# Routing tables by wide compares, and the last of the down weights' norms worked out inside the first tile

## What is computed

```python
x = x + xattn(layernorm(x), ctx)            # keys from ctx, similarity, layer norm over it, softmax
n = layernorm(x)
scores = n @ Wg.T                           # 8 experts
topk_s, topk_i = top_k(scores, 2);  probs = softmax(topk_s)
for e in range(8):                          # H = 352
    h = silu(n @ W1[e].T) * (n @ W2[e].T)
    y = y + w[..., e:e+1] * (h @ W3[e].T)
x = x + y
```

## Time and profile before

| what | value |
|---|---|
| median of 3 runs | 388.02 us (388.01 to 388.85) |
| the profiled execution's own time | 388.37 us |
| its span | 386.6 us |
| PE, DVE, ACT, POOL busy | 357.8, 272.8, 263.4, 163.6 us |
| mean granted PE clock | 0.961 of full |

### The profile page before, as it was taken

How to read it: one execution, slowest core, us unless ns; L and a number is a source line. 1 busy time by engine, 2 the same in 40 slices (tenths; PEclk the granted TensorE clock), 3 DMA queues, 4 the chain that set the end, 5 groups by cost and what they waited for, 6 DMA issues and landing times.

```text
span 386.6 us, 8316 instructions
## 1 busy us (share of the span) xinstructions
PE 357.8 (93%) x2317; PEld 235.7 (61%) x2317; DVE 272.8 (71%) x725; ACT 263.4 (68%) x455; POOL 163.6 (42%) x200
## 2 busy tenths in 40 slices
PE   8998999978979778889999999999999999999981
PEld 7554576756946445556666666666666666666640
DVE  2367788988796999995757676666767575757660
ACT  2388999966684988976666657575666666665750
POOL 2124748557334134545253434444343435253331
PEclk9999999998559899999999999999999999999998
DMA  6999999999412133355544445353535354544524
GB/s 226 412 409 401 323 412 388 367 339 357 162 19 66 31 54 57 54 86 88 103 68 98 77 91 84 82 89 77 101 67 109 61 105 68 98 76 91 81 31 54
DMA packets 21947, 57.62 MB, mean 149 GB/s; under 512 B 4816, under 2 KB 4944, under 8 KB 20368
## 3 DMA queue, kind: packets, MB, share of 16 engines
q0 software_dynamic: 8736, 20.53, 30.0%
q1 hardware_dynamic: 12016, 30.27, 20.8%
q10 hardware_dynamic: 1152, 6.29, 4.6%
HBM read 38.17 MB, written 18.91 MB: 148 GB/s over the span
## 4 chain that ended last, share of the span: by engine, by line
PE 73%; DVE 10%; issue 5%; ACT 4%; DMA 4%; POOL 2%; POOLq 0%; ACTq 0%; DVEq 0%
PE bank L1236 34%; PE bank L1270 17%; PE bank L1094 4%; PE bank L1227 4%; PE bank L1028 3%; PE bank L1256 3%; PE bank L1136 3%; DMA stage<-in_xT 2%; DVE stage L784 2%; PE bank L1114 2%; DVE stage L786 1%; DVE Wp L812 1%; PE bank L1121 1%; DMA out<-kvj_s,sidx 1%; ACT stage L660 1%
## 5 line engine op out<-in xcount | busy, mean ns | idle before, releaser
L967 DVE SCALAR_TENSOR_TENSOR stage<-W,w3sc,stage 128x512 f16<-128x512 f16 x117 | 84.2, 748 | 6.5 <-ACT stage L660 6.5
L1270 PE MATMUL bank<-stage,n_s 128*128 128x512 f16 (+1 forms) x351 | 82.2, 379 | 1.8 <-issue 1.5
L1236 PE MATMUL bank<-Wp,kvg_s 128*128 x480 | 78.2, 313 | 3.5 <-DVE kvg_s L973 3.5
L660 ACT ACTIVATE stage<-W,w3sc 128x512 f16 x117 | 80.1, 717 | 0.0
L1236 PE MATMUL bank<-Wp,kv_s 128*128 x456 | 75.9, 317 | 4.2 <-DVE kv_s L973 4.2
L506 POOL DMA_INDIRECT out<-oT_s,sidx x20 | 34.1, 1706 | 75.4 <-ACT oT_s L687 68.3
L1236 PEld LDWEIGHTS bank<-Wp,kvg_s 128*128 128x128 f16 x480 | 46.7, 98 | 29.6 <-issue 5.1
L1236 PEld LDWEIGHTS bank<-Wp,kv_s 128*128 128x128 f16 x456 | 44.9, 99 | 29.8 <-issue 5.5
L991 DVE TENSOR_TENSOR n_s<-bank,n_s 128x384 f16<-128x384 f32 x39 | 21.7, 557 | 55.1 <-ACT n_s L673 55.1
L506 POOL DMA_INDIRECT out<-kvj_s,sidx x19 | 32.4, 1707 | 65.7 <-ACT kvj_s L687 63.1
L1270 PEld LDWEIGHTS bank<-stage,n_s 128*128 128x128 f16 (+1 forms) x351 | 34.2, 98 | 35.1 <-issue 2.3
(11 more groups left out here) (184 smaller groups left out, 554.5 us busy)
## 6 DMA issues: line engine op xcount, KB each, us to landing
Wp<-in_w SPq DMA_DIRECT2D x8, 1408.0 KB, 10.8
W<-in_w ACTq DMA_DIRECT2D x8, 768.0 KB, 7.7
stage<-in_xT SPq DMA_DIRECT2D x4, 1024.0 KB, 9.8
W<-in_x SPq DMA_DIRECT2D x12, 256.0 KB, 10.9
out<-W SPq DMA_DIRECT2D x12, 256.0 KB, 8.7
n_table<-n_s SPq DMA_DIRECT2D x8, 256.0 KB, 7.2
n_table<-x_s SPq DMA_DIRECT2D x8, 256.0 KB, 5.5
stage<-in_x SPq DMA_DIRECT2D x4, 256.0 KB, 9.4
```

Source lines behind the costliest of these rows:

```text
L660: eng.activation(w3p[t % 2][:, c * D:(c + 1) * D], W3[:, bass.ds(e * W3N + c * D, D)], ACT.Copy, scale=w3sc[:, bass.ds(e, 1)]).then_inc(s_ ...
L967: eng.scalar_tensor_tensor(w3p[r][:, W3N + c * D:W3N + (c + 1) * D], W3[:, bass.ds(e * W3N + c * D, D)], w3sc[:, bass.ds(e, 1)], w3p[r][:, ...
L1236: mm = eng.matmul(bank[2 * which + r][:, 0:H], n_, w_, start=(c == 0 and k == 0), stop=(c == DC - 1 and k == 2))
L1270: mm = eng.matmul(ybank(t - 1)[:, :], h_, w_, start=(c == 0 and k == 0), stop=(c == HC - 1 and k == 2))
```

## The change

`columns(0..2)` become two DVE instructions each: one compare of 128x1024 against the ramp for `oh_r` and one for `oh_c`, with 16-bit copies of ri and qi repeated along the last axis. The multiplication by the row number moves to ACT as `number(q)`, four in-place activations of 128x256. Groups 3 and 4 stay as they were.

Order: `scale_in(15)` goes one slot ahead; `columns(0)` goes from slot 14 to slot 16, `places(1)` from 15 to 17, `columns(1)` from slot 16 to behind slot 17, `weight_sums` from 14 to 15, `weight_scale` from slot 16 to behind `chosen(12)`, POOL's `weight_root` from slot 14 to slot 17 (behind `norm(15)`). On ACT `w3_square(0)` goes from slot 14 to 15 and `w3_square(1)` behind `number(2)`; squares 6 and 7 go into `tile(0)`, with a junk buffer of their own. The matmul for W3's norms goes into PE's `tile(1)`, and `w3_sums`, `w3_scale` and the weights of tile 0's rows go into DVE's `tile(0)`, behind the gate and half a `w12_low`; ACT waits for `w3sc` in `w3_high` and no longer ahead of `tile(0)`. Fewer `warm` matmuls: 24 for 36 beside the gather, 8 for 12 in slots 14 and 15. The diff, cut to its core (`gate` and `row_weights` hold the instructions of L981 to L988 and L996 to L999, unchanged):

```diff
 W3_ORDER = (4, 5, 6, 7, 0, 1, 2, 3)
+W3_LATE = 6
 W3_LOAD_SLOT = (11, 12, 13, 14, 14, 15, 15, 16)
-WARM_GATHER = 36
+WARM_GATHER = 24
...
-WARM_LAST = 12
+WARM_LAST = 8
...
+WIDE = 3
...
+        rf16 = sb("rf16", [P, G * TOPK], F16)
+        qf16 = sb("qf16", [P, G * TOPK], F16)
...
+        w3junk.append(stage[:, DC * N:DC * N + W3N // 2].bitcast(BF16))
...
                     eng.memset(zrow[:, :], 0.0).then_inc(s_zr, 1)
-                if s == 14:
+                if s == 17:
...
-                if s in (14, 15):
-                    w3_square(s - 14)
+                if s == 15:
+                    w3_square(0)
+                if s == 16:
+                    number(0)
...
-                eng.activation(w3junk[k > 1], W3[:, e * W3N:(e + 1) * W3N], ACT.Square, accum_out=w3sq[:, e:e + 1]).then_inc(s_w3q, 1)
+                eng.activation(w3junk[(k > 1) + (k >= W3_LATE)], W3[:, e * W3N:(e + 1) * W3N], ACT.Square, accum_out=w3sq[:, e:e + 1]).then_inc(s_w3q, 1)
...
+            def number(q):
+
+                eng.wait_ge(s_ohp, q + 1)
+                for i in range(TPB):
+                    cols = slice(i * TOPK, (i + 1) * TOPK)
+                    eng.activation(oh_r[:, q % 2, cols, :], oh_r[:, q % 2, cols, :], ACT.Copy,
+                                   scale=tok1[:, q * TPB + i:q * TPB + i + 1]).then_inc(s_ohn, 1)
...
             turned(G - 2)
             router_exp(0)
+            number(1)
             turned(G - 1)
+            number(2)
+            w3_square(1)
             w12_high(0, 0)
+            w12_high(0, 1)
             w3_square(2)
-            w12_high(0, 1)
             w3_square(3)
             router_exp(1)
             eng.activation(spare_a[:, 1:2], half[:, :], ACT.Silu)
-            for k in range(4, E):
+            for k in range(4, W3_LATE):
...
                     wait(eng, s_yp, t - 1)
+                    eng.wait_ge(s_w3sc, 1)
                     eng.activation(w3p[t % 2][:, c * D:(c + 1) * D], W3[:, bass.ds(e * W3N + c * D, D)], ACT.Copy,
...
                 if t == 0:
                     mT_evac(1)
+                    for k in range(W3_LATE, E):
+                        w3_square(k)
+                    w12_high(EARLY, 0)
                 w3_high(t, e, 0)
-                w12_high(t + EARLY, 0)
+                if t > 0:
+                    w12_high(t + EARLY, 0)
                 w3_high(t, e, 1)
                 if t > 0:
                     mT_evac(t + 1)
...
-            eng.wait_ge(s_w3sc, 1)
...
-                eng.tensor_copy(rf[:, cols], ri[:, cols]).then_inc(s_rqf, 1)
+                eng.tensor_copy((rf16 if q < WIDE else rf)[:, cols], ri[:, cols]).then_inc(s_rqf, 1)
                 eng.wait_ge(s_rq, 2 * q + 2)
-                eng.tensor_copy(qf[:, cols], qi[:, cols]).then_inc(s_rqf, 1)
+                eng.tensor_copy((qf16 if q < WIDE else qf)[:, cols], qi[:, cols]).then_inc(s_rqf, 1)
...
+                if q < WIDE:
+                    cols, ring, shape = slice(g0 * TOPK, (g0 + m) * TOPK), slice(i0, i0 + m * TOPK), [P, m * TOPK, P]
+                    eng.tensor_tensor(oh_r[:, a, ring, :], ramp[:, 0:1, :].to_broadcast(shape),
+                                      rf16[:, cols, None].to_broadcast(shape), ALU.is_equal).then_inc(s_ohp, 1)
+                    eng.tensor_tensor(oh_c[:, a, ring, :], ramp[:, 0:1, :].to_broadcast(shape),
+                                      qf16[:, cols, None].to_broadcast(shape), ALU.is_equal).then_inc(s_ohc, 1)
+                    return
...
-                if row(s):
+                if row(s) and s < G - 1:
...
+                if s == G - 2:
+                    scale_in(G - 1)
+                if s == 16:
+                    columns(0)
+                if s == 17:
+                    places(1)
...
-                if s == 14:
+                if s == 15:
                     weight_sums()
...
-                if s == 14:
-                    columns(0)
-                if s == 15:
-                    places(1)
-                if s == 16:
-                    weight_scale()
-                    columns(1)
...
+            columns(1)
             chosen(G - 4)
+            weight_scale()
             places(2)
             chosen(G - 3)
...
+            def row_weights(t, e):
...
+            def gate(t, e):
...
+                    if t > 0:
+                        row_weights(t, e)
...
-                    if t == 0:
-                        low_rows(1)
-                    w3_low(t, e, 0)
...
+                    if t > 0:
+                        w3_low(t, e, 0)
+                    gate(t, e)
                     w12_low(t + EARLY, 0)
                     if t > 0:
                         low_rows(t + 1)
+                    else:
+                        w3_sums()
+                        w3_scale()
+                        eng.wait_ge(s_yinv, 1)
+                        row_weights(t, e)
+                        w3_low(t, e, 0)
                     w3_low(t, e, 1)
                     w3_low(t, e, 2)
                     w12_low(t + EARLY, 1)
...
             w12_low(0, 1)
             low_rows(0)
-            w3_sums()
             w12_low(1, 0)
-            w3_scale()
             w12_low(1, 1)
-            eng.wait_ge(s_yinv, 1)
+            low_rows(1)
             for t in range(NT + 1):
                 tile(t)
...
+                if q < WIDE:
+                    eng.wait_ge(s_ohn, g0 + m)
+                    eng.wait_ge(s_ohc, q + 1)
                 for c in range(m * TOPK):
-                    eng.wait_ge(s_ohr, g0 * TOPK + c + 1)
-                    eng.wait_ge(s_ohc, g0 * TOPK + c + 1)
+                    if q >= WIDE:
+                        n = (g0 - GROUPS[WIDE][0]) * TOPK + c + 1
+                        eng.wait_ge(s_ohr, n)
+                        eng.wait_ge(s_ohc, WIDE + n)
...
-                if s == 15:
-                    table(0)
...
             rank(2)
             router(G - 3)
+            table(0)
             turn_n(G - 1)
             router(G - 2)
+            rank(3)
             table(1)
-            rank(3)
             router(G - 1)
-            table(2)
             rank(4)
             counts()
+            table(2)
             table(3)
             warm(wide, WARM_DRAIN // 2)
...
+                if t == 1:
+                    eng.wait_ge(s_w3q, E)
+                    eng.wait_ge(s_ti, G + 1)
+                    eng.matmul(bank[4][:, 0:E], ones[:, :], w3sq[:, :], start=True, stop=True).then_inc(s_w3qp, 1)
...
-            eng.wait_ge(s_w3q, E)
-            eng.wait_ge(s_ti, G + 1)
-            eng.matmul(bank[4][:, 0:E], ones[:, :], w3sq[:, :], start=True, stop=True).then_inc(s_w3qp, 1)
```

More of the change, by code:

```diff
@@ L254, in build @@
         s_r = sem("s_r")
-        s_oh, s_cs, s_rank, s_cntp, s_pick, s_pos, s_rq, s_rqf, s_ohr, s_ohc, s_tab, s_sel, s_tabT, s_gp, s_et, s_eoff, s_esp, s_jcol = [
-            sem(n) for n in ("s_oh", "s_cs", "s_rank", "s_cntp", "s_pick", "s_pos", "s_rq", "s_rqf", "s_ohr", "s_ohc", "s_tab",
+        s_oh, s_cs, s_rank, s_cntp, s_pick, s_pos, s_rq, s_rqf, s_ohp, s_ohn, s_ohr, s_ohc, s_tab, s_sel, s_tabT, s_gp, s_et, s_eoff, s_esp, s_jcol = [
+            sem(n) for n in ("s_oh", "s_cs", "s_rank", "s_cntp", "s_pick", "s_pos", "s_rq", "s_rqf", "s_ohp", "s_ohn", "s_ohr", "s_ohc", "s_tab",
                              "s_sel", "s_tabT", "s_gp", "s_et", "s_eoff", "s_esp", "s_jcol")]
@@ L974, in low_rows @@
                                              ALU.subtract).then_inc(s_ml, 1)
+            def row_weights(t, e):
+                r = t % 2
+                eng.wait_ge(s_ng[t % 3], 16 * (t // 3 + 1))
+                wait(eng, s_wm, t)
+                eng.tensor_scalar(wsel[:, :], ng[t % 3][:, D + 2:D + 4], ecol[:, t:t + 1], yinv[:, bass.ds(e, 1)],
+                                  ALU.is_equal, ALU.mult).then_inc(s_ws, 1)
+                eng.wait_ge(s_ws, t + 1)
+                wait(eng, s_y, t - 1)
+                eng.tensor_tensor_reduce(wmul[:, :], wsel[:, :], ng[t % 3][:, D:D + 2], 1.0, 0.0, ALU.mult, ALU.add,
+                                         wm[:, r:r + 1]).then_inc(s_wm, 1)
+            def gate(t, e):
+                r = t % 2
+                eng.wait_ge(s_a, t + 1)
+                eng.wait_ge(s_bp, t + 1)
+                wait(eng, s_hTp, t - 1)
+                eng.scalar_tensor_tensor(hid[r], bank[2 + r][:, 0:H], winvh[:, bass.ds(e, 1)], act_a[r], ALU.mult, ALU.mult).then_inc(s_h, 1)
             def tile(t):
@@ L980, in tile @@
                     e = eng.value_load(ecoli[0:1, t:t + 1], min_val=0, max_val=E - 1)
-                    eng.wait_ge(s_ng[t % 3], 16 * (t // 3 + 1))
-                    wait(eng, s_wm, t)
-                    eng.tensor_scalar(wsel[:, :], ng[t % 3][:, D + 2:D + 4], ecol[:, t:t + 1], yinv[:, bass.ds(e, 1)],
-                                      ALU.is_equal, ALU.mult).then_inc(s_ws, 1)
-                    eng.wait_ge(s_ws, t + 1)
-                    wait(eng, s_y, t - 1)
```

(4 more changed lines are left out.)

4 lines of the change are left out of this document (removed).

## The result

395.48 us, the median of 4 runs (393.45 to 398.52), against 388.02 before in the same comparison (388.01 to 388.85): a ratio of 1.0192 with a 95% interval of 1.0147 to 1.0238. The change makes the kernel slower by 7.5 us. The forecast was 390.5, with a range of 386.4 to 392.8: the direction was right, the size was not, and the time lies outside the range. The profiled execution took 395.03 us with a span of 393.3; its mean granted clock of PE, 0.960, is that of before.

A forecast was written before the change was run, and what follows sets the result against it. PE's fixed beat from 168 us on passes on any shift of DVE's first hidden low part. -2.2 + 4.3 + 0.3 = +2.4, with roundings +2.5 us, gave 390.5 us on the median's scale; range 386.4 to 392.8.

The forecast's parts named there:

- part 4: Gather: the last weights' store releases it instead of gidx, at 112.9; first product at 118.7, 2.2 us earlier.
- part 5: Tile 0: from first product to DVE's first hidden low part 16.6 us instead of 12.25, costing 4.3 us.
- Part 1: DVE's tables: wide compares take 1.2 us each, a group 2.4 instead of 3.2; ACT's number takes 1.6 a group.
- Part 2: Row group 15: residual at 87.3, POOL's norms blocked by wide compares, rows 15 ready at 94.0, 3.2 us earlier.
- The rival without blocking: POOL's norms slip in before the compares: rows 15 ready at 91.2, 387.7 us, no difference; chance 0.25.
- Part 3: Root of the weights' norms behind norm(15) on POOL, weight_scale and places(2) waiting: ACT's number(2) starts at 99.4.
- Landing takes 3.6: After the gather's start: its rows take 3.6 us to land, as in the earlier trace.
- the first product 2.1 later: In front of tile 0: the first expert product starts 2.1 us after rows 0 are transposed, at 118.7.
- the -2.2 of the sum: Before the first expert product: it starts 2.2 us earlier than in the kernel before.
- The rest: Other moves give nothing; PE's wait before the first down products adds 0.3 us, with 0 to 2.5 as ends.
- a rival of chance 0.15: PE's clock: idle before the gathered rows land and before tile 0's down products costs more, 392 to 393.5 us; chance 0.15.
- The last rival: Routing: the tables leave the last rows' path, but the last weights' path stays as long; inside the forecast.

The follow-up runs named there:

- e7: The changed kernel with columns(1) moved behind weight_scale, so that no wide compare meets norm(15); 396.15 us.
- e2: The kernel before with only W3's part of the change, squares 6 and 7 and the whole chain in tile 0; 392.47 us.
- e5: The changed kernel with W3's part undone, router_exp(1) early and 36 warm matmuls beside the gather; 389.06 us, ratio 1.0016.
- e8: The changed kernel with narrow compares, W3's part undone, and 36 and 12 warm matmuls; 388.29 us.
- e9: e5 with two fills of wide warm matmuls, ten and twelve, where PE waits for DVE in the last rows; 387.50 us.
- e12: The changed kernel with narrow compares, W3's part undone, fills of 10 and 5, 36 warm matmuls, router_exp(1) behind w12_high(0, 1); 387.50 us.
- e11: e9 with a second fill of 5 for 12 and the eviction of rows 0 ahead of w12_high(1, 0); 385.27 us, ratio 0.9912.
- e1: The changed kernel with W3's part undone, all eight squares, sum, root and scale ahead of tile 0 again; 389.72 us.
- e10: The changed kernel with only the two fills of warm matmuls, ten and twelve, added; 393.26 us.
- e3: The changed kernel with ACT's router_exp(1) moved to straight behind w3_square(1); 389.50 us.
- e4: The changed kernel with 60 warm matmuls for 24 beside the gather; 394.27 us.
- e6: The changed kernel in its new order with narrow compares and without number on ACT; 394.40 us.

## Why the prediction was wrong, and where it was right

The terms of the sum gave +2.4 us, the two spans differ by 6.7. The missing 4.3 are 2.3 in front of the first product (part 4), 1.2 in tile 0 (part 5), 0.2 in the first down products and 0.6 in the one late gather.

**Part 1 held.** The compares take 1.21 to 1.24 us (forecast 1.2 from start to start, measured 1.14 to 1.16); `number` takes 1.69 for four (1.6). The Trainium skill, "Vector Engine (DVE) Microarchitecture Reference", section 5.1, has two rules here. The trace agrees with the second, one element a cycle for an input that is read over and over: by the first a compare would have taken about 0.65.

**Part 2 held in its mechanism, and in its time with some luck.** Rows 15 were ready at 93.99 (94.0), but by two misses that cancel: their residual started at 88.20 and not at 87.7, and from there it took 5.79 us and not 6.24. That a wide compare holds POOL's instruction is shown, by 2.31 against 0.77 in e7. The Trainium skill's rule in "SBUF — State Buffer", "Who interferes with whom", would have all four compares block, and the trace agrees: both norms lie across two compares and end behind the second. Each was held for about 1.5 us, where I had 0.4 for `norm(13)` and 2.4 for `norm(15)`. `norm(13)` kept residual 15 waiting only 0.27 us, and `norm(14)`, queued behind it, let `norm(15)` begin at 90.50, half a microsecond after ACT's sum of squares (89.81 + 0.19). The rival without blocking is out.

**Part 3 held.** `number(2)` at 99.33 (99.4), with DVE standing 1.85 us for the root.

**Part 4 held up to the gather's start and failed behind it.** `router_exp(1)` 108.44 (108.5), `gidx` 109.06 (109.4), gather 113.15 (112.9). The step that failed is "Landing takes 3.6": it was taken from the earlier trace rows, where no `w12_low` ran beside the first gather's instruction. I had moved the gather's release away from `gidx` and didn't look at what DVE starts behind `gidx`: two `w12_low`, from 111.06 on. Beside them the first gather instruction takes 2.30 us for 1.25, and from start to transposes 4.80. That is 1.0 to 1.1 us. Then "the first product 2.1 later" was 3.0, because PE had stood 4.53 us: the transposes took 0.5 more, and the ten `warm` matmuls behind them, 2.34 us for 1.25, ended later than DVE's part of the rows and held the product up. With 0.25 from the gather's start that makes 121.0 for 118.7: the whole of the -2.2 of the sum went here.

**Part 5 held for the chain** (16.85 in e2, 16.6 forecast) and missed what PE's clock adds in it, 0.9 for the first product: 17.73.

**The rest was mis-sized.** PE's clock stood in the sum with 0.3 and in a rival of chance 0.15 that made it 1.5 to 3 us more. Measured are 0.9 before the first product, 0.9 in it and, behind 8.24 us without work, 1.9 in the first down products, of which 0.5 lasts to the next product (6.05 - 5.59). I had PE stand some 2 us before the rows land, and priced the clock by the row of 3.52 instead of 1.96 after 2.21 us. My own figures gave more: 24 of 36 `warm` matmuls at 6.36 us are 4.2, from 109.2 on, so they end 3.2 us before 116.6; it came to 4.53. And after waits of 2.03 to 2.21 us the clock went either way: twelve products took 3.52 in before and 1.96 in e5, e8, e9 and e12, nine down products 2.1 in e8 and e9, 2.8 in e11 and 3.8 in e5 and e12. After the longer waits in front of the same work it was low each time: 3.80 to 4.79 us before the rows' transposes (after, e1, e7, e10: 1.08 or 1.09 us for 0.60), 8.24 or 8.25 before the down products (seven traces: 3.41 to 4.00). Even so, the down products' price isn't always passed on: in e2 and e3, at 3.41 and 3.47, the next product came 4.04 us behind the gauge, as in before. The sum with measured terms: +0.1 (first product) + 5.5 (tile 0) + 0.5 (down products) + 0.6 (late gather and its aftermath) = 6.7, the difference of the spans. The last rival, that the path of the last weights stays as long, was part of the forecast and came true: the gather starts at 113.15 for 113.28, and e3 shows that the store held it.

What stays open: why the clock falls in some executions and in others not, at the same wait of 1.8 us for `chosen(10)` in the last rows. Runs of after lie between 393.45 and 398.52; the 0.8 us between the 7.5 of the medians and the 6.7 of the spans is only which executions were profiled. That the clock makes the scatter isn't shown: the kernel before scatters by 2.5 to 4.5 us in the later comparisons, and in e10 two runs with the same mean clock, 0.964, took 392.66 and 396.07. What the width of the compares is worth by itself is open too (e12).

## What to carry to other kernels

When a change brings one of two inputs of a step forward, price the other one from its new place in its queue, and then look again at what runs beside the step at its new time: here `gidx` came 3.7 us earlier, the gather 0.1, and the first product not at all. A chain (norms, root, scale) moved out of a stretch where an engine waits anyway into the first tile of a beat saves nothing there and costs 4.6 us here (16.85 for 12.25 in e2). Where PE is to stand before work on the path, work out how long from the rows, and price that work at the lower clock: in front of the transposes and the down products it was low after each wait of 3.8 us and more here, and after some of those of 2.0 to 2.2. And compare kernels within one comparison, changing one thing: after and e4, e5 and e9, e11 and e12 look further apart by their medians than they can be shown to be, or for more than one reason.

## What the runs showed of the hardware

GpSimd's indirect DMA is held by a DVE operation with two inputs from SBUF just as a norm is. Where the first gather is issued while a `w12_low` (128x1408) runs, its instruction takes 2.15 to 2.40 us instead of 1.25, and ends 1.11 or 1.12 us after that operation's end (both operations together take 3.28, and the gather begins 0.4 to 0.6 us into the second):

```
kernel   gather starts, takes, ends   the two w12_low end   between
after    113.15  2.30  115.45         111.06 + 3.28 = 114.34   1.11
e1       113.36  2.18  115.54         111.14 + 3.28 = 114.42   1.12
e4       115.84  2.16  118.00         113.61 + 3.28 = 116.89   1.11
e7       114.36  2.15  116.51         112.12 + 3.28 = 115.40   1.11
e10      114.08  2.40  116.48         112.08 + 3.28 = 115.36   1.12
```

It waits for one operation, not for both: in e6 the second gather meets the first of two, takes 2.23 for 0.96 and ends 0.84 us behind that one's end. ACT isn't what holds it: in e6 ACT stood from 112.1 to 115.22. POOL's timeline of e6, then DVE's, in which the first of the two ends at 113.42 + 1.68 = 115.10:

```profile
112.16 1.25 POOL L497 DMA_INDIRECT ng_s<-n_table,gidx  x1 [3.02 <-DVE sidx L969]
113.71 2.23 POOL L497 DMA_INDIRECT ng_s<-n_table,gidx  x1 [0.30 <-issue]
```

```profile
113.42 3.28 DVE L838 SCALAR_TENSOR_TENSOR Wp<-Wp,wscale 128x1408 f16<-128x1408 f32 x2
```

The Trainium skill, "SBUF — State Buffer", "Who interferes with whom", supposes, as an inference, that an operation with two inputs doesn't hold the making of DMA descriptors. These rows differ from it; they decide. What in the instruction is held isn't shown. The third gather of before falls in line: it begins at 116.09, late in the first `w12_low` (114.80 + 1.68 = 116.48), takes 1.22 for 0.96 and ends 0.83 behind it. But a gather that begins within 0.03 us of such an operation isn't held: the first of before (113.28) takes its 1.25 beside a two-input compare of 320 elements from 113.28 on, the second (114.83) its 0.96 beside the `w12_low` from 114.80 on.

PE's clock can cost twice over: 60 `warm` matmuls instead of 24 beside the gather gave 1.8 us back in front of and in the first product (one trace of each), and with 10 wide `warm` matmuls at a wait of about 1.8 us in the last rows the granted clock from 86 to 98 us was 0.97 to 1.00 in the three traces with wide compares (e9 to e11), where the six without such a fill have 0.61 to 0.98.
